# Additive attention with two-of-eight experts: expert pairs over two PSUM banks, another choice of the two experts, and another step table

## The reference, cut to what matters

```python
# attention of layer L2, on the normalised x; 64 units
k = x @ Wx
q = x @ Wt
h = jnp.tanh(q[:, :, None, :] + k[:, None, :, :] + bt)
e = jnp.exp(jnp.einsum('bijq,qo->bij', h, Wa) + ba[0])
s = jnp.sum(e, axis=-1, keepdims=True)
v = jnp.einsum('bij,bjd->bid', e / (s + EPS), x)
# experts of layer L2, on the normalised result; E = 8, H = 256, K = 2
logits = flat @ router_w.T
topk_vals, topk_idx = jax.lax.top_k(logits, K)
topk_w = jax.nn.softmax(topk_vals, axis=-1)
dense_w = jnp.zeros((s, E), dtype=flat.dtype).at[jnp.arange(s)[:, None], topk_idx].add(topk_w)
g = jnp.einsum('sd,edh->esh', flat, w_gate)
u = jnp.einsum('sd,edh->esh', flat, w_up)
y = jnp.einsum('esh,ehd->esd', jax.nn.silu(g) * u, w_down)
out = jnp.einsum('esd,se->sd', y, dense_w)
```

## Time and profile before

| | us |
|---|---|
| median of 3 runs | 2241.42 (2240.25 to 2244.61) |
| profiled execution, its own time | 2243.55 |
| its span in the trace | 2241.8 |
| this stage, first argument to last sum | 679.88 to 1834.92 |
| PE, DVE, ACT busy over the whole span | 1822.3, 1744.4, 1320.1 |

### The profile page before, as it was taken

How to read it: one execution, slowest core, us unless ns; L and a number is a source line. 1 busy time by engine, 2 the same in 40 slices (tenths; PEclk the granted TensorE clock), 3 DMA queues, 4 the chain that set the end, 5 groups by cost and what they waited for, 6 DMA issues and landing times. The chain is left out here.

```text
span 2241.8 us, 31865 instructions
## 1 busy us (share of the span) xinstructions
PE 1822.3 (81%) x11804; PEld 936.1 (42%) x11804; DVE 1744.4 (78%) x4911; ACT 1320.1 (59%) x1467; POOL 305.1 (14%) x360
## 2 busy tenths in 40 slices
PE   6989998897865688999989999889999889754930
PEld 3556655675421133334333344333443364332620
DVE  3677457778768789999999999999999879785532
ACT  1322122241337999999999999999999821110410
POOL 6000012000442000000000000000000000057046
PEclk9898999896878999999999999999999999877965
DMA  5501000000001100000000000000000000031732
GB/s 167 184 1 38 11 8 14 1 1 1 1 1 36 66 1 1 1 1 1 1 1 1 1 1 1 1 1 1 1 1 1 1 1 1 0 142 52 232 107 75
DMA packets 45803, 65.00 MB, mean 29 GB/s; under 512 B 7744, under 2 KB 35920, under 8 KB 44880
## 3 DMA queue, kind: packets, MB, share of 16 engines
q1 hardware_dynamic: 39472, 48.25, 6.4%
q0 software_dynamic: 6176, 14.71, 2.3%
HBM read 37.77 MB, written 23.07 MB: 27 GB/s over the span
## 5 line engine op out<-in xcount | busy, mean ns | idle before, releaser
L2017 ACT ACTIVATE KM<-KM 128x2048 f32<-128x2048 f32 x290 | 539.1, 1911 | 8.0 <-DVE KM L1840 8.0
L1840 DVE TENSOR_SCALAR KM<-big 128x512 f32<-128x512 f32 x1160 | 479.7, 479 | 37.8 <-PE bank L2155 30.9
L2155 PE MATMUL bank<-KM,w_a_wa 128*32 128x512 f32 x2736 | 375.7, 623 | 96.3 <-ACT KM L2017 73.9
L191 POOL TENSOR_TENSOR nrstd<-nrstd,minus_half 128x4 f32<-128x4 f32 (+1 forms) x80 | 82.5, 1052 | 1719.8 <-DVE nrstd L168 1719.6
L2017 ACT ACTIVATE aa_args<-aa_args 128x2048 f32<-128x2048 f32 x142 | 266.3, 1911 | 1.5 <-DVE aa_args L1840 1.5
L1840 DVE TENSOR_SCALAR aa_args<-big 128x512 f32<-128x512 f32 x568 | 235.6, 478 | 13.8 <-PE bank L2155 13.2
L2155 PE MATMUL bank<-aa_args,w_a_wa 128*32 128x512 f32 x1360 | 186.7, 622 | 43.1 <-ACT aa_args L2017 29.2
L2155 PEld LDWEIGHTS bank<-KM,w_a_wa 128*32 128x32 f32 x2736 | 54.5, 109 | 243.2 <-ACT KM L2017 140.9
L2014 ACT ACTIVATE KM<-big 128x512 f32<-128x512 f32 x208 | 132.9, 719 | 0.0
L2121 PE MATMUL bank_pair<-XT,rf_wgu 128*128 128x256 f32 x320 | 88.3, 398 | 0.8 <-DVE ST L1912 0.8
L2127 PE MATMUL bank_pair<-XT,rf_wgu 128*128 128x256 f32 x320 | 88.2, 398 | 0.0
(11 more groups left out here) (452 smaller groups left out, 3260.2 us busy)
## 6 DMA issues: line engine op xcount, KB each, us to landing
queues<-zeros SPq DMA_DIRECT2D x1, 8192.0 KB, 24.1
KM<-queues SPq DMA_DIRECT2D x32, 256.0 KB, 3.7
results<-KM SPq DMA_DIRECT2D x32, 256.0 KB, 3.4
w<-in_w SPq DMA_DIRECT2D x1, 4096.0 KB, 12.9
mf_tv<-in_task_W SPq DMA_DIRECT2D x1, 2048.0 KB, 9.1
la_v<-in_task_W SPq DMA_DIRECT2D x1, 2048.0 KB, 7.7
big<-XN SPq DMA_DIRECT2D x8, 256.0 KB, 2.7
rf_wgu<-in_wgu SPq DMA_DIRECT2D x1, 2048.0 KB, 8.3
```

The lines of the kernel that those rows point to most:

```text
L191: self.nc.gpsimd.tensor_tensor(self.m.nrstd[s][:, 0:self.tiles], self.m.nrstd[s][:, 0:self.tiles], self.m.minus_half[:, 0:self.tiles], ALU ...
L1840: last = nc.vector.tensor_scalar(ARG(n, step)[:, cc, :], KU[:, i * T:(i + 1) * T], q, None, ALU.add)
L2017: last = nc.scalar.activation(ARG(n, step), ARG(n, step), ACT.Tanh)
L2155: last = nc.tensor.matmul(m.bank[g][32 * cc:32 * cc + 32, :], w["a_wa"][:, 30 - 2 * k:62 - 2 * k], ARG(n, step)[:, cc, :], start=k == 0, s ...
```

## The change

Four things, all in this stage.

- Experts go in pairs v = 0 to 3. Both gates of a pair are written to one pair of banks and both factors to the other, so tanh and the two multiplications are single instructions of 128x1024. There is one buffer of tanh results, one of products, and one output bank. A pair begins at step 17, 25, 33 or 41; its matmuls for the second expert stand one step behind the first.
- In the drain the pairs of the last tile begin 4 steps apart, and the last pair of the tile before it 4 steps after the third. For these the last tile's odd pairs have a second product buffer and a second output bank.
- The two experts of a token are found by an instruction for the eight largest values and one for their places, for each of the two tiles of 128 tokens, where a chain of eleven instructions, each waiting for the one before, stood. Two multiplications by the weights become one.
- `BIASED` has four steps and not five, and `TURN_X`, `COPY_X`, `ROUTE`, `LOGITS`, `E2`, `EXP` and `SHARES` stand one or two steps later.

```diff
@@ -1658,39 +1658,37 @@
 class Top2:
...
+        self.ramp = m.w["ramp"][:, 64 - E:64].rearrange("p (o e) -> p o e", o=1).broadcast_to([P, 2 * rows, E])
+
+    def over(self, v):
+        return v.rearrange("p (n o) -> p n o", o=1).broadcast_to([P, 2 * self.rows, self.E])
+
+    def values(self, dve, i, logits):
+        nc = self.nc
+        for t in range(self.rows):
+            last = nc.vector.max(self.v8[:, t, :], logits[:, t, :])
+        last.then_inc(self.step.sem, 1)
+        dve.wait_ge(self.step.sem, self.step.at(i, 1))
+
+    def places(self, dve, i, logits):
+        nc = self.nc
+        for t in range(self.rows):
+            last = nc.vector.max_index(self.i8[:, t, :], self.v8[:, t, :], logits[:, t, :])
+        last.then_inc(self.step.sem, 1)
+        dve.wait_ge(self.step.sem, self.step.at(i, 2))
+        nc.vector.tensor_scalar(self.place[:, :].rearrange("p (k n) -> p n k", k=2), self.i8[:, :, 0:2],
+                                -1.0, float(self.E), ALU.mult, ALU.add).then_inc(self.step.sem, 1)
+        dve.wait_ge(self.step.sem, self.step.at(i, 3))
+        nc.vector.tensor_tensor(self.oh[:, :, :], self.ramp, self.over(self.place[:, :]), ALU.is_equal).then_inc(self.step.sem, 1)
...
-    BIASED = (8, 12, 16, 22, 23)
+    BIASED = (8, 15, 17, 24)
...
-    START = 20
-    begin = lambda e: START + 3 * e
-    UP, TANH, MUL, LIFTED, DOWN, SUM = 1, 2, 6, 7, 5, 12
+    EP = E // 2
+    COUNT = PAIRS * NC_
+    LAST = COUNT - 1
+    START = 17
+    BEGIN, BEGIN_DRAINED, BEGIN_LAST = (17, 25, 33, 41), (17, 25, 33, 37), (17, 21, 25, 29)
+    begin = lambda j, v: (BEGIN_LAST if j == LAST else BEGIN_DRAINED if j == LAST - 1 else BEGIN)[v]
+    GATED, UP, TANH, MUL, LIFTED, DOWN, SUM = (0, 1), (2, 3), 3, 7, 8, (6, 7), (14, 15)
...
-    TH = lambda e: m.ST[0][:, e % 2, :]
-    ACB = [m.t512b[0][:, :], m.t512b[1][:, :], m.ST[1][:, 0, :], m.ST[1][:, 1, :]]
-    AC = lambda e: ACB[e % 4]
+    TH = m.ST[0][:, 0:2, :]
+    AC = lambda j, v: m.t512c[0][:, 0:2, :] if j == LAST and v % 2 else m.ST[1][:, 0:2, :]
...
-    GATE, LIFT = (lambda v: m.bank[3 + 2 * v % 3]), (lambda v: m.bank[3 + (2 * v + 1) % 3])
-    OUT = lambda e: m.bank[6 + e % 2][:, 0:2 * D]
+    gate_ps, up_ps, th_sb, a1_sb, ac_sb = (sig(n, EP) for n in ("gate_ps", "up_ps", "th_sb", "a1_sb", "ac_sb"))
+    dn, h_sb = sig("dn", EP), sig("h_sb", E)
+    GATE, LIFT = m.bank_pair
+    OUT = lambda j, v, x: m.bank[2 if j == LAST and v % 2 else 3][:, x * 2 * D:(x + 1) * 2 * D]
+    held = lambda j, v: 1 if j == LAST and v else 0
...
-    NORM, TURN_X, COPY_X, ROUTE, LOGITS, E2, EXP, SHARES = 13, 12, 13, 15, 21, 22, 18, 25
+    NORM, TURN_X, COPY_X, ROUTE, LOGITS, E2, EXP, SHARES = 13, 13, 15, 16, 22, 23, 20, 27
...
                     nc.vector.tensor_copy(lg[:, :, :], m.bank[2][:, 0:2 * E].rearrange("p (n e) -> p n e", e=E)).then_inc(lg_sb.sem, 1)
                 if step == e2_at:
                     dve.wait_ge(lg_sb.sem, lg_sb.at(j, 1))
-                    top.vector(dve, j, lg[:, :, :])
-
-                    nc.vector.tensor_tensor(e2[:, :], top.v[:, 1, :], top.v[:, 0, :], ALU.subtract).then_inc(e2_in.sem, 1)
+                    top.values(dve, j, lg[:, :, :])
+                    nc.vector.tensor_tensor(e2[:, :], top.v8[:, :, 1], top.v8[:, :, 0], ALU.subtract).then_inc(e2_in.sem, 1)
+                    top.places(dve, j, lg[:, :, :])
...
+                    nc.vector.tensor_tensor(top.oh[:, :, :], top.oh[:, :, :], top.over(share[:, :]), ALU.mult).then_inc(wstep.sem, 1)
                     dve.wait_ge(wstep.sem, wstep.at(j, 4))
-                    nc.vector.tensor_tensor(WT[:, :, :], WT[:, :, :], top.oh[1][:, :, :], ALU.add).then_inc(w_sb.sem, 1)
+                    nc.vector.tensor_tensor(WT[:, :, :], top.oh[:, 0:2, :], top.oh[:, 2:4, :], ALU.add).then_inc(w_sb.sem, 1)
                     dve.wait_ge(w_sb.sem, w_sb.at(j, 1))
...
             def units(j, step):
...
+                for v in begun(j, step, MUL):
+                    dve.wait_ge(th_sb.sem, th_sb.at(j, v + 1))
+                    nc.vector.scalar_tensor_tensor(TH, TH, 1.0, GATE[:, :, :], ALU.add, ALU.mult).then_inc(a1_sb.sem, 1)
+                for v in begun(j, step, LIFTED):
+                    dve.wait_ge(a1_sb.sem, a1_sb.at(j, v + 1))
+                    dve.wait_ge(up_ps.sem, up_ps.at(j, v + 1))
+                    if v or j:
+                        dve.wait_ge(dn.sem, dn.at(j, v - held(j, v)))
+                    nc.vector.tensor_tensor(AC(j, v), TH, LIFT[:, :, :], ALU.mult).then_inc(ac_sb.sem, 1)
+                for x in range(2):
+                    for v in begun(j, step, SUM[x]):
+                        e = 2 * v + x
+                        dve.wait_ge(dn.sem, dn.at(j, v + 1))
+                        if e:
+                            dve.wait_ge(h_sb.sem, h_sb.at(j, e))
+                        for s in S:
+                            h = m.h[:, tile_of(j) + s * NC_, :]
+                            last = nc.vector.scalar_tensor_tensor(h, OUT(j, v, x)[:, s * D:(s + 1) * D], WT[:, s, e:e + 1], h, ALU.mult, ALU.add)
+                        last.then_inc(h_sb.sem, 1)
...
             def units(j, step):
...
+                for v in begun(j, step, TANH):
+                    act.wait_ge(gate_ps.sem, gate_ps.at(j, v + 1))
+                    if v or j:
+                        act.wait_ge(ac_sb.sem, ac_sb.at(j, v))
+                    nc.scalar.activation(TH, GATE[:, :, :], ACT.Tanh, scale=0.5).then_inc(th_sb.sem, 1)
...
             def units(j, parity, step):
...
+                for x in range(2):
+                    for v in begun(j, step, DOWN[x]):
+                        e = 2 * v + x
+                        if x == 0:
+                            pe.wait_ge(ac_sb.sem, ac_sb.at(j, v + 1))
+                            if v or j:
+                                pe.wait_ge(h_sb.sem, h_sb.at(j, e - 2 * held(j, v)))
+                            if j == LAST and v == 1:
+                                pe.wait_ge(lg_sb.sem, lg_sb.at(j, 1))
+                        for s in S:
+                            for a in range(HB):
+                                o = a * TOK + s * P
+                                last = nc.tensor.matmul(OUT(j, v, x)[:, s * D:(s + 1) * D], AC(j, v)[:, x, o:o + P], wd[:, e, a, :],
+                                                        start=a == 0, stop=a == HB - 1)
+                        if x:
+                            last.then_inc(dn.sem, 1)
+                    for v in begun(j, step, UP[x]):
+                        e = 2 * v + x
+                        if x == 0 and (v or j):
+                            pe.wait_ge(ac_sb.sem, ac_sb.at(j, v))
                         for a in range(HB):
+                            last = nc.tensor.matmul(LIFT[:, x, a * TOK:(a + 1) * TOK], wgu[:, e, 1, a, :], XMT[parity][:, 0:TOK], start=True, stop=True)
+                        if x:
+                            last.then_inc(up_ps.sem, 1)
+                    for v in begun(j, step, GATED[x]):
+                        e = 2 * v + x
+                        if x == 0 and (v or j):
+                            pe.wait_ge(a1_sb.sem, a1_sb.at(j, v))
+                        for a in range(HB):
+                            last = nc.tensor.matmul(GATE[:, x, a * TOK:(a + 1) * TOK], wgu[:, e, 0, a, :], XMT[parity][:, 0:TOK], start=True, stop=True)
+                        if x:
+                            last.then_inc(gate_ps.sem, 1)
```

More of the change, by code:

```diff
@@ L1658, with __init__ @@
 class Top2:
-    STEPS = 11
-    def __init__(self, ctx, nc, m, tag, rows, E, per=1):
+    STEPS = 4
+    def __init__(self, ctx, nc, m, tag, rows, E):
         self.nc, self.rows, self.E = nc, rows, E
-        self.eq = ctx.sb(tag + "_t2_eq", [P, rows, E])
-        self.rest = ctx.sb(tag + "_t2_rest", [P, rows, E])
-        self.oh = [ctx.sb(f"{tag}_t2_oh{n}", [P, rows, E]) for n in range(2)]
-        self.v = ctx.sb(tag + "_t2_v", [P, 2, rows])
-        self.r = ctx.sb(tag + "_t2_r", [P, 2, rows])
-        self.step = Signal(ctx, nc, tag + "_t2_step", self.STEPS)
-        self.ramp = m.w["ramp"][:, 64 - E:64].rearrange("p (o e) -> p o e", o=1).broadcast_to([P, rows, E])
@@ L1674, in vector @@
[L1674 to L1693 removed]
+        self.v8 = ctx.sb(tag + "_t2_v", [P, rows, 8])
@@ new lines, in __init__ @@
+        self.i8 = ctx.sb(tag + "_t2_i", [P, rows, 8], U32)
+        self.place = ctx.sb(tag + "_t2_place", [P, 2 * rows])
+        self.oh = ctx.sb(tag + "_t2_oh", [P, 2 * rows, E])
+        self.step = Signal(ctx, nc, tag + "_t2_step", self.STEPS)
+        self.ramp = m.w["ramp"][:, 64 - E:64].rearrange("p (o e) -> p o e", o=1).broadcast_to([P, 2 * rows, E])
[7 more added lines that the diff above has]
+        dve.wait_ge(self.step.sem, self.step.at(i, 1))
```

81 lines of the change are left out of this document (8 added, 73 removed).

## The result

The changed kernel takes 2204.73 us in the median (2201.46 to 2208.43, 4 runs), the kernel before on the same chip 2243.02 (2240.25 to 2245.39, 4 runs): a ratio of 0.983, interval 0.981 to 0.985. The forecast was 2199, its range 2190 to 2224. The profiled execution took 2208.43 us, its span 2206.5.

The account below looks back on a forecast made before the run. It took ACT to bound the stage, with waits for PE adding 2.4 us per cycle. Steady part -45.8, iteration 0 -0.65, tail -0.3 and drain +4.0 sum to -42.7, from median 2241.42 to 2199 us; range 2190 to 2224.

Parts of the forecast that it names:

- ACT's work: Steady cycles: one biased step made plain saves 0.65 us, merged tanh 0.2, leaving 65.4 per cycle.
- rival 3: Tanh of pairs: merging saves the whole fixed part, 0.17 us each instead of 0.05; total 2192; chance 0.05.
- ACT's waits: Steady cycles: ACT's three waits for PE go and no others come, -2.4 us per cycle.
- rival 1: Steady cycles: PE still comes late and waits return; 2232 us at full cost, 2215 at half; chance 0.19.
- step 12: Tightest place, tanh of pair 3: ACT wants it at 23.7 us, PE done at 23.56 plus 0.1, so no wait.
- the steady part: Fourteen cycles between small exponentials: from 68.67 to 65.4 us, 3.27 less each, -45.8 in all.
- DVE as cover: Steady cycles: DVE's work stays about 63.3 us per cycle, below ACT's 65.4, so ACT never waits for DVE.
- Rival 2: Steady cycles: DVE stands waiting for tanh at all four pairs, cycle 69.7 us, total 2258; chance 0.08.
- Iteration 0: Outside the steady cycles: one biased step less, -0.65 us.
- The tail of iteration 15: Exponential to last step: one biased step less (-0.65) against two tanh of 0.90 for three of 0.47 (+0.4), -0.3 us.
- The drain: After the last attention step: PE waits 3 us before the values, last tile's first gate at 25.0, end at 54.2, +4.0.
- Sum and time: All terms together: -42.7 us on the stage, giving 2199 us from the median of 2241.42.

Follow-up runs that it names:

- e2: The changed kernel with five biased steps (8, 12, 15, 17, 24) instead of four; cycle 66.02 us, ratio to before 0.983.
- e4: The changed kernel with three biased steps (8, 15, 24) instead of four; cycle 65.21 us, ratio to before 0.979.
- e3: The changed kernel with the old eleven-instruction choice of experts; cycle 65.67 us, ratio to before 0.977.
- e8: e6 with three biased steps and the small exponential at step 22 instead of 20; cycle 64.762 us, whole time 2217.03 us.
- e9: e3 with the small exponential at step 22 instead of 20; cycle 65.338 us, ratio to before 0.983.
- e5: The kernel before with four biased steps (8, 12, 16, 22) and all else as it was; cycle 68.28 us, ratio to before 0.999.
- e1: The changed kernel with the pairs of the last two tiles 8 steps apart like all others; drain 65.53 us, ratio to before 0.980.
- e6: The changed kernel with the values' copy, division, last tile's parts and small exponential earlier in the drain; drain 54.55 us, whole time 2211.25 us, ratio to before 0.977.

## Why the prediction was right, step by step

- **ACT's work (65.4 per cycle): right.** The trace has 65.346. That a biased step is worth 0.65 is shown by e2 (+0.68). The merged tanh costs 0.91 to the next start, forecast 0.90, so four pairs save 0.2 and rival 3 is out: the fixed part of a PSUM tanh was almost wholly hidden already. The Trainium skill (VectorE: DVE Perf Modes, "The TRN2 errata") says of SBUF latency that it is exposed between instructions, once for each. Applied to these tanh, whose source is PSUM, as rival 3 does, it prices too high: 0.47 for 512 and 0.91 for 1024 leave, less 0.8 ns per element as in the earlier trace rows, under 0.1 exposed in each. With an SBUF source the trace doesn't speak against it: the four instructions of 512 of a biased step take 2.45 where one of 2048 takes 1.80, 0.22 for each instruction more; they have a bias as well, so what part is the instruction's the runs do not tell.
- **ACT's waits (-2.4): right, rival 1 is out, by little.** The place with no reserve, step 12, holds: not one wait in the view. The trace shows how near it was. The count has 23.7 against 23.56 and 0.1, nothing to spare; measured it is 0.25 us more than the bare hand-over at first and nothing in the last five cycles, which cost 0.02 to 0.03 us each. The forecast of the steady part rested on this count, and that it was kept at a margin of zero is in part luck. At pairs 0, 1 and 2 the distances are 1.5 to 1.7, 0.5 to 0.8 and 0.8 to 1.1, where the forecast has 0.5 to 1.6.
- **DVE as cover: right for this kernel, the reserve was overrated.** 63.0 of work per cycle against 63.3. Rival 2 is out: DVE stands 29.0 us in fourteen cycles for tanh, 2.1 per cycle, only at two pairs and only with time in hand. But the reserve that I read as 65.4 - 63.3 = 2.1 us can't be spent at will. A biased step fewer (e4) takes 1.5 of it and loses 0.5 of its 0.65 gain, because DVE is late at one instruction; the old choice (e3), 1.1 more of DVE's work, costs 0.32 at the same one. With that deadline two steps later both are free (e8, e9).
- **Iteration 0 (-0.65): too small, by 2.9.** The second and third projection copy of ACT waited 1.72 and 1.90 us for PE before and 0.37 each after. I had not walked iteration 0 at all: PE has fewer parts there, but ACT waits for it too. It does not stem from the number of biased steps: e2, with five, has the short waits too (0.37 at the second, 2.7 us for the three copies together), and e5, the kernel before with four, the long ones (1.73 at the second, 5.4 together, 5.5 in before). So the pairs or the step table did it; which of them was not tried.
- **The tail of iteration 15 (-0.3): right.**
- **The drain (+4.0): the mechanism right, the size half of the +8.6.** This is the term that was most mis-sized. The way the prediction put it, PE waits 3 us for the late copy and starts the values at 10.1. It did: 3.37 us of wait, 10.7. But the values were then priced at full clock. At the granted 0.50 to 0.71 they and pair 3's gates took 3.32 + 2.35 in place of 2.15 + 1.89, 1.6 us more, and the tanh of pair 3 was at 16.2 instead of 13.8: 0.6 late start, 1.6 clock, 0.2 rest. The gate of the last tile came at 28.2, +3.2, which is 0.8 more on the way there, not split. Behind it come 1.4 more, and those are DVE's work: from its first multiplication (1770.82) to the end there are 27.5 us, of which 4.2 are holes and 23.3 work, where the forecast has 4.1 and 22. The holes forecast as 0.8, 1.4, 1.8 and 0.9 stand as 0.69, 1.29, 1.60 and 0.71, and a fifth, 0.62 for the tanh of pair 1, was not foreseen. e1 and e6 show the remedy and its size: closer pairs -6.8, copy and tile earlier -4.2.
- **Sum and time.** Two errors of opposite sign, -2.9 and +4.6, and a cycle 0.05 better, 14 times, leave the stage 1.1 off. The sum was nearer than its terms deserved, and that is luck. The other 4.7 us to the median are not the stage's: in the two profiled executions the rest of the kernel differs by 6.4 us.
